# A mixture-of-experts feed-forward by halves of the tokens, with resident weights and shares spread by DMA

## Chip, cores, metric

The kernel runs on one core of a Trainium2 chip. The metric is the device time of one execution in microseconds (us). Before the change it is 1184.66 us, the median of 3 runs (1184.16 to 1185.03).

## What is computed

Four layers act on x of shape 2 x 1024 x 128 (2048 tokens, 128 channels, float32), each added to x and each working on a layer norm of it:

```
x = x + attention(norm(x))      # 16 heads, learned distance bias
x = x + ffn(norm(x))            # F1
x = x + mamba(norm(x))          # x + inner residual
x = x + ffn(norm(x))            # F2, the same weights as F1

ffn(xf):
  scores = sigmoid(xf @ router_w.T)          # 64 experts
  sfc    = scores + correction_bias
  keep the 4 of 8 groups with the best sum of two; the best 8 experts of those
  c      = scores of the chosen / (their sum + 1e-20) * 2.5, zero elsewhere
  routed = sum over e of c[:, e] * (square(relu(xf @ up_w[e])) @ down_w[e])   # hidden 64
  shared = square(relu(xf @ shared_up_w)) @ shared_down_w                     # hidden 256
  return routed + shared
```

Every expert is computed for every token; c is zero for those not chosen.

## The kernel before, in words

Tokens lie in 16 tiles of 128 rows, four quarters of 512. Each layer is a stage (`attention`, `moe_ffn` with the tag f1, `mamba`, `moe_ffn` with f2), with a barrier of all engines between stages. All engines run their own program and wait on semaphores.

**Feed-forward (`moe_ffn`, line 214).** The layer norm (lines 171 to 182) normalizes 16 tiles on VectorE; TensorE transposes them; ACT copies them rounded to fp32r (line 445, the high part) and POOL subtracts to get the low part (line 508). TensorE makes the logits (line 354), ACT the sigmoid (line 451), and VectorE routes all 16 tiles (lines 524 to 567), ending in shares c in two f16 parts, which TensorE transposes to cT (line 388). Meanwhile the two shared pieces run as eight units (lines 457, 461, 365).

The 64 experts are 32 pairs, so that a pair's hidden width is 128. A routed unit is one pair and one quarter, 128 units a stage, in loops of 24 (`each_unit`). In a unit TensorE does three fp32r matmuls up (high x high, low x high, high x low: lines 360 to 362), three down for the unit four back (line 401), and one that spreads the two experts' shares over 64 partitions each, by a one-hot matrix `m.spread` times cT (line 417). ACT does the relu (line 478) and casts the high part of act (line 471); VectorE multiplies relu by the share (line 585) and the product by the hidden value again (line 591), which gives c times the square; POOL subtracts for the low part (line 514). SP loads each pair's weights (lines 320 and 324) into two slots; ACT casts their high parts (lines 484, 492) and VectorE subtracts for the low ones (line 573). So the order in a unit is relu, share product, second product, cast, low part, down.

At the end ACT copies the sums (line 499), TensorE turns them back (line 428), VectorE adds x (line 600) and, in f2, SP stores the output by quarters (line 339).

**Attention (line 752)** goes by steps (ALL_STEPS). SP's queue holds, step by step, the maxima (line 915), tables of the bias and the stacks of q and k; POOL copies v once in a while (line 979). **Mamba**: ACT writes each of 16 units of the projection into a padded buffer (line 1534), VectorE convolves it by three instructions (line 1689); POOL's softplus (lines 1621 to 1627) follows ACT's last copy and VectorE's reciprocal (line 1697).

## Time and profile before

| what | value |
|---|---|
| median of 3 runs | 1184.66 us |
| the profiled execution | 1184.06 us |
| its span | 1182.1 us |
| mean granted TensorE clock | 0.933 |
| busy: TensorE / VectorE / ACT / POOL | 86% / 83% / 61% / 38% |

The span runs from the first instruction to the last; the profiled execution's own time lies 2 us above it. A clock of 1.00 is TensorE's full speed. "Share" of DMA is the mean busy share of the core's 16 DMA engines. All rows are from this one execution. "Idle before" is how long an engine stood still before an instruction, and the name behind the arrow is what ended the wait.

### The profile page before, as it was taken

The page shows a single profiled execution, that of the slowest core. Times are in us where ns is not written, and L with a number is a line of the kernel's source. Part 1 is how long each engine was busy: PE and PEld are TensorE (multiplying, and loading weights), DVE is VectorE, ACT ScalarE, POOL GpSimd, SP SyncE. Part 2 cuts the span into 40 slices and gives each one's busy share as a digit, 9 for nine tenths or more (in the row PEclk, how much of TensorE's full clock was granted, in tenths as well). Part 3 has the DMA queues.
Part 4 walks back from the last instruction along what each step waited for, and adds up shares of the span by engine and source line. Part 5 has one row for each costly group of instructions (what it writes and reads, how often), then busy time and mean ns, then how long its engine had stood idle before and what let it go on. Part 6 is the DMA issues. An engine that isn't in the chain of part 4 may idle for free. (4 is left out here: it accounts for less than half of the span.)

```text
span 1182.1 us, 19693 instructions
## 1 busy us (share of the span) xinstructions
PE 1020.0 (86%) x5756; PEld 540.9 (46%) x5756; DVE 983.5 (83%) x2432; ACT 719.0 (61%) x1175; POOL 447.7 (38%) x404
## 2 busy tenths in 40 slices
PE   3559999999999999785999999782877769999998
PEld 1212222222222222264766676541656537666775
DVE  6589999889999986168999999787876689999997
ACT  5116665666666656564777777586333537777775
POOL 4600000000000000013777778515663127777776
PEclk9659999999999999967999999986889879999999
DMA  3740122032012200000000000000000000000001
GB/s 100 255 95 8 61 76 49 16 106 66 15 55 75 57 1 2 1 21 12 20 21 18 22 18 23 3 19 0 1 0 0 21 9 21 22 18 21 19 23 38
DMA packets 56704, 41.66 MB, mean 35 GB/s; under 512 B 23334, under 2 KB 51004, under 8 KB 56636
## 3 DMA queue, kind: packets, MB, share of 16 engines
q1 hardware_dynamic: 54268, 38.18, 12.0%
q10 hardware_dynamic: 2368, 2.63, 0.8%
q8 instruction: 36, 0.59, 0.2%
q14 instruction: 32, 0.26, 0.1%
HBM read 33.12 MB, written 7.47 MB: 34 GB/s over the span
## 5 line engine op out<-in xcount | busy, mean ns | idle before, releaser
L514 POOL TENSOR_TENSOR f_act_low<-f_act,f_act_high 128x512 fp32r<-128x512 f32 x256 | 331.2, 1294 | 151.3 <-ACT f_act_high L471 146.3
L1203 ACT ACTIVATE at_prob<-at_cols 128x1024 f32<-128x1024 f32 x256 | 248.1, 1021 | 198.4 <-PE at_cols L1092 198.4
L1255 DVE CUSTOM_DVE_ANT_0 at_rows<-at_rows,at_table_max 128x512 f32<-128x512 f32 x512 | 340.3, 719 | 33.5 <-PE at_rows L1057 32.3
L471 ACT CAST f_act_high<-f_act 128x512 fp32r<-128x512 f32 x256 | 159.1, 621 | 68.1 <-DVE f_act L591 65.7
L585 DVE TENSOR_TENSOR f_gated<-f_relu,f_work 128x512 f32<-128x512 f32 x256 | 174.3, 681 | 21.3 <-PE f_work L417 15.1
L591 DVE TENSOR_TENSOR f_act<-f_gated,f_work 128x512 f32<-128x512 f32 x256 | 175.8, 687 | 10.2
L478 ACT ACTIVATE f_relu<-f_work 128x512 f32<-128x512 f32 x256 | 152.9, 597 | 32.1 <-PE f_work L362 30.7
L360 PE MATMUL f_work<-f_x_high,f_wu_high 128*128 128x512 f32 x256 | 148.4, 580 | 2.7 <-DVE f_wu_low L573 2.1
L1057 PE MATMUL at_rows<-at_k_stack,at_q_stack 48*128 48x512 bf16 x512 | 104.7, 405 | 39.9 <-DVE at_maxima L1255 38.4
L1104 PE MATMUL at_pv<-at_prob,at_v_stack 128*32 128x512 f32 x1024 | 136.4, 605 | 0.6 <-ACT at_prob L1203 0.6
L1092 PE MATMUL at_cols<-at_table_cols,flip_sum 128*64 128x512 f16 x1024 | 136.4, 387 | 0.0
L979 POOL COPY at_v_stack<-at_v_nat 128x256 f32<-128x256 f32 x8 | 3.1, 400 | 333.1 <-PE at_pv L1104 333.1
L1057 PEld LDWEIGHTS at_rows<-at_k_stack,at_q_stack 48*128 48x128 bf16 x512 | 24.9, 93 | 189.2 <-DVE at_maxima L1255 150.1
L401 PE MATMUL f_acc<-f_act_high,f_wd_high 128*128 128x512 f32 x256 | 102.2, 399 | 2.4 <-POOL f_act_low L514 2.4
L417 PE MATMUL f_work<-f_cT,spread 128*128 128x512 f16 x256 | 100.9, 394 | 2.5 <-DVE f_gated L585 2.3
L361 PE MATMUL f_work<-f_x_low,f_wu_high 128*128 128x512 f32 x256 | 101.7, 397 | 0.0
L362 PE MATMUL f_work<-f_x_high,f_wu_low 128*128 128x512 f32 x256 | 101.6, 397 | 0.0
L401 PE MATMUL f_acc<-f_act_high,f_wd_low 128*128 128x512 f32 x256 | 101.5, 397 | 0.0
L401 PE MATMUL f_acc<-f_act_low,f_wd_high 128*128 128x512 f32 x256 | 101.5, 396 | 0.0
L1085 PE MATMUL at_cols<-at_q_stack,at_k_stack 51*128 51x512 bf16 x512 | 78.8, 379 | 2.6 <-ACT at_prob L1203 2.6
L1092 PEld LDWEIGHTS at_cols<-at_table_cols,flip_sum 128*64 128x64 f16 x1024 | 49.0, 109 | 63.7 <-issue 38.8
L1255 DVE DVE_READ_ACCUMULATOR2_ANT at_maxima<- 128x1 f32 x512 | 72.8, 142 | 0.0
(274 smaller groups left out, 1393.8 us busy)
## 6 DMA issues: line engine op xcount, KB each, us to landing
at_table_cols<-bias_rows SPq DMA_DIRECT2D x32, 248.0 KB, 5.1
at_table_max<-bias_rows SPq DMA_DIRECT2D x12, 480.0 KB, 4.3
f_wu<-in_L_ffn_up_w_dram SPq DMA_DIRECT2D x64, 64.0 KB, 2.0
f_wd<-in_L_ffn_down_w_dram SPq DMA_DIRECT2D x64, 64.0 KB, 1.8
at_q_stack<-q_parts SPq DMA_DIRECT2D x28, 96.0 KB, 2.4
at_k_stack<-k_parts SPq DMA_DIRECT2D x24, 96.0 KB, 3.9
at_table_max<-bias_rows ACTq DMA_DIRECT2D x4, 480.0 KB, 5.8
k_parts<-at_parts SPq DMA_DIRECT2D x2, 768.0 KB, 5.4
```

Source lines behind the costliest of these rows:

```text
L360: mm(hid[:, n % 3, :], w_hi, xh[:, cols], start=True, stop=False)
L401: last = mm(acc[:, j % 4, :], w[:, slot, :], x[:, j % 4, :], start=False, stop=(k == 2), skip_group_check=True)
L471: nc.scalar.copy(act_h[:, j % 4, :], act[:, j % 4, :]).then_inc(act_high, 1)
L478: nc.scalar.activation(relu[:, j % 2, :], hid[:, j % 3, :], ACT.Relu).then_inc(relu_ready, 1)
L514: nc.gpsimd.tensor_tensor(act_l[:, k, :], act[:, k, :], act_h[:, k, :].bitcast(F32), ALU.subtract).then_inc(act_low, 1)
L585: tt(gated[:, j % 2, :], relu[:, j % 2, :], cw, ALU.mult).then_inc(gate_done, 1)
L591: tt(act[:, j % 4, :], gated[:, j % 2, :], hid[:, j % 3, :], ALU.mult).then_inc(act_ready, 1)
L1057: last = mm(s1[:, (at + j) % SLOTS, :], q_st[r, p.b, p.lh, p.hp, p.lbq * P:(p.lbq + 1) * P], k_st[r, p.b, p.hp, p.mh * BANK:(p.mh + 1) * B ...
L1092: last = mm(s2[u * HALF:(u + 1) * HALF, hp, j, :], m.flip_sum[:], t_col[:, 2 * hp + j, c:c + BANK], start=False, stop=True)
L1104: last = mm(pv[32 * h:32 * h + 32, :], vst[:, it % 2, LT - 1 - s % LT, h, :], prob[:, S % 2, h, :], start=(s % LT == 0), stop=(s % LT == L ...
L1203: act(prob[:, S % 2, 2 * hp:2 * hp + 2, :], s2[:, hp, :, :], ACT.Exp).then_inc(exp_done, 1)
L1255: nc.vector.tensor_tensor_reduce(out=slot, in0=slot, in1=t_max[:, 2 * p.hp + j, c:c + BANK][:, ::-1], scale=1.0, scalar=-3.0e38, op0=ALU.a ...
```

## The change

**Weights.** In attention SP loads all weights of the feed-forward in nine pieces (the shared ones, then eight of four pairs, two DMAs each) into a double buffer, at steps 4, 16, 28 and so on. Two steps later POOL splits each into high and low parts, two copies and two subtractions for a piece. They stay in SBUF for both feed-forward stages. Some of attention's early tensors share their space. The constants `spread` and `ident16` go.

**Halves.** A stage runs two halves of 1024 tokens. Each has a head (norm, logits, routing for 8 tiles), 68 units (34 pairs, the two shared pieces among them, by two quarters) and a tail. The head of half 0 runs alone, on all engines; the head of half 1 is woven into half 0's units at numbered places, the tail of half 0 into half 1's. The programs are written out instead of looped.

**Shares.** c becomes its square root: ACT's Sqrt, then a step of Newton on VectorE. TensorE turns it (four float32 transposes), ACT copies it, SP stores it to DRAM (`c_rows`, one row of 512 tokens for a quarter and an expert). Then each routed unit has one DMA that reads two rows of 2 KB, repeats each over 64 partitions, and writes the 128 x 512 tile `cw` in one of six slots. A slot's load waits for the gate (VectorE's product) six units back; half 1's first six wait for all gates of half 0. VectorE makes max(hidden, 0) times the root of the share in one instruction, ACT squares it and casts the high part, POOL takes the low part. The matmul that spread the shares is gone.

**Mamba.** The padded buffer holds one sequence instead of two, so ACT's copies for the second wait for convolutions of the first; `yg` shares its space with `sz`.

The core of the diff:

```diff
+def allot_weights(m):
+    m.wu_h, m.wu_l = (m.sb(f"wu_{k}", [D, NPAIRS, P], F32R) for k in ("high", "low"))
+    m.wd_h, m.wd_l = (m.sb(f"wd_{k}", [P, NPAIRS, D], F32R) for k in ("high", "low"))
...
+def weave(main, side):
+    side = iter(side)
+    due = next(side, None)
+    for k, _ in enumerate(main):
+        while due is not None and due <= k + 1:
+            due = next(side, None)
+    while due is not None:
+        due = next(side, None)
...
+AT_ROOT, AT_ROWS, AT_TURN, AT_COPY, AT_HIGH, AT_LOW, AT_LOGITS = 2, 3, 5, 6, 7, 8, 8
+AT_SCORE, AT_ROUTE = 12, 13
+AT_C_ROOT, AT_NEWTON, AT_C_TURN, AT_C_COPY = 38, 39, 42, 43
+AT_TAIL = 8
...
+        def sp_shares(sp, b):
+            h = halves[b]
+            sp.wait_ge(h.rcT_ready, 1)
+            sp.dma_start(c_rows[QH * b:QH * (b + 1)].rearrange("q e t -> (q e) t"), rcT[:]).then_inc(h.rc_out, 16)
+            sp.wait_ge(h.rc_out, 16)
+            for n in range(SHARED * QH, FFN_UNITS):
+                k, e = n - SHARED * QH, 2 * (n // QH - SHARED)
+                if k >= C_SLOTS:
+                    sp.wait_ge(h.gate_done, n - C_SLOTS + 1)
+                elif b:
+                    sp.wait_ge(halves[0].gate_done, FFN_UNITS)
+                sp.dma_start(cw[:, k % C_SLOTS, :], c_rows[QH * b + n % QH, e:e + 2, :].unsqueeze(1)
+                             .broadcast_to([2, HID, BANK])).then_inc(h.c_in[k % C_SLOTS], 16)
+                yield
...
+        def pe_units(pe, b):
+            h = halves[b]
+            def up(n):
+                pp, cols = n // QH, slice((QH * b + n % QH) * BANK, (QH * b + n % QH + 1) * BANK)
+                if n == 0:
+                    pe.wait_ge(h.x_low, QH)
+                    if b:
+                        pe.wait_ge(halves[0].gate_done, FFN_UNITS)
+                if n >= 2:
+                    pe.wait_ge(h.gate_done, n - 1)
+                for k, (w, x) in enumerate(((m.wu_h, xh), (m.wu_h, xl), (m.wu_l, xh))):
+                    last = nc.tensor.matmul(hid[:, n % 2, :], w[:, pp, :], x[:, cols], start=(k == 0), stop=(k == 2))
+                last.then_inc(h.up_done, 1)
+            def down(n):
+                pp, s = n // QH, n % PART_SLOTS
+                pe.wait_ge(h.low_done, n + 1)
+                for k, (w, x) in enumerate(((m.wd_h, act_h), (m.wd_h, act_l), (m.wd_l, act_h))):
+                    last = nc.tensor.matmul(acc[:, QH * b + n % QH, :], w[:, pp, :], x[:, s, :],
+                                            start=(pp == 0 and k == 0), stop=(pp == NPAIRS - 1 and k == 2),
+                                            skip_group_check=True)
+                last.then_inc(h.down_done, 1)
+            for n in range(FFN_UNITS + LAG):
+                if n < FFN_UNITS:
+                    up(n)
+                if n >= LAG:
+                    down(n - LAG)
+                yield
...
+        def act_units(a, b):
+            h = halves[b]
+            def high(n):
+                a.wait_ge(h.square_done, n + 1)
+                if n >= PART_SLOTS:
+                    a.wait_ge(h.down_done, n - PART_SLOTS + 1)
+                elif b:
+                    a.wait_ge(halves[0].down_done, FFN_UNITS)
+                nc.scalar.copy(act_h[:, n % PART_SLOTS, :], act[:, n % ACT_SLOTS, :]).then_inc(h.high_done, 1)
+            for n in range(FFN_UNITS):
+                a.wait_ge(h.gate_done, n + 1)
+                if n >= ACT_SLOTS:
+                    a.wait_ge(h.low_done, n - ACT_SLOTS + 1)
+                elif b:
+                    a.wait_ge(halves[0].low_done, FFN_UNITS)
+                nc.scalar.activation(act[:, n % ACT_SLOTS, :], gated[:, n % 3, :], ACT.Square).then_inc(h.square_done, 1)
+                if n:
+                    high(n - 1)
+                yield
+            high(FFN_UNITS - 1)
...
+        def pool_units(pool, b):
+            h = halves[b]
+            for n in range(FFN_UNITS):
+                pool.wait_ge(h.high_done, n + 1)
+                nc.gpsimd.tensor_tensor(act_l[:, n % PART_SLOTS, :], act[:, n % ACT_SLOTS, :],
+                                        act_h[:, n % PART_SLOTS, :].bitcast(F32), ALU.subtract).then_inc(h.low_done, 1)
+                yield
...
+            tt(masked[:], masked[:], wsum[:, 0, :].unsqueeze(2).broadcast_to([P, HT, E_ALL]), ALU.mult).then_inc(h.c_ready, 1)
+            yield AT_NEWTON
+            v.wait_ge(h.root_ready, 1)
+            ch.link(ts(sfc[:], root[:], 1e-18, None, ALU.max))
+            ch.link(nc.vector.reciprocal(sfc[:], sfc[:]))
+            yield AT_NEWTON + 1
+            ch.link(tt(sfc[:], sfc[:], masked[:], ALU.mult))
+            ch.link(tt(sfc[:], sfc[:], root[:], ALU.add))
+            yield AT_NEWTON + 2
+            if b:
+                v.wait_ge(halves[0].rcT_done, 1)
+            ts(rc[:].rearrange("p k a e -> p a k e"), sfc[:].rearrange("p (a k) e -> p a k e", a=QH), 0.5, None,
+               ALU.mult).then_inc(h.rc_ready, 1)
+        def dve_units(v, b):
+            h = halves[b]
+            for n in range(FFN_UNITS):
+                v.wait_ge(h.up_done, n + 1)
+                if n >= 3:
+                    v.wait_ge(h.square_done, n - 2)
+                elif b:
+                    v.wait_ge(halves[0].square_done, FFN_UNITS)
+                if n < SHARED * QH:
+                    ins = nc.vector.tensor_scalar(gated[:, n % 3, :], hid[:, n % 2, :], 0.0, None, ALU.max)
+                else:
+                    k = n - SHARED * QH
+                    v.wait_ge(h.c_in[k % C_SLOTS], 16 * (k // C_SLOTS + 1))
+                    ins = nc.vector.scalar_tensor_tensor(out=gated[:, n % 3, :], in0=hid[:, n % 2, :], scalar=0.0,
+                                                         in1=cw[:, k % C_SLOTS, :], op0=ALU.max, op1=ALU.mult)
+                ins.then_inc(h.gate_done, 1)
...
+        def stage_program(head, units, tail, eng):
+            run(head(eng, 0))
+            weave(units(eng, 0), head(eng, 1))
+            weave(units(eng, 1), tail(eng, 0))
+            run(tail(eng, 1))
...
+                sp.dma_start(rw[:], router_w).then_inc(rw_in, 16)
+                sp.dma_start(cbias[:], correction_bias.rearrange("(a e) -> a e", a=1).broadcast_to([P, E_ALL])).then_inc(cbias_in, 16)
+                run(sp_shares(sp, 0))
+                if out is None:
+                    run(sp_shares(sp, 1))
+                else:
+                    weave(sp_shares(sp, 1), sp_store(sp, 0))
+                    run(sp_store(sp, 1))
+                    for h in halves:
+                        sp.wait_ge(h.stored, 16 * QH)
...
-                def unit(i, j):
-                    slot = j // 4 % 2
-                    if j % 4 == 0:
-                        pe.wait_ge(w_low, 6 * i + (j // 4 + 1))
-                    if past(i, j, 3):
-                        pe.wait_ge(act_ready, BODY * i + (j - 2))
-                    up(wu_h[:, slot, :], wu_l[:, slot, :], j % 4, j)
-                    if past(i, j, LAG):
-                        down_routed(i, j - LAG)
-                    if past(i, j, 1):
-                        pe.wait_ge(gate_done, BODY * i + j)
-                    e = 12 * i + 2 * (j // 4)
-                    mm(cw, m.spread[:, bass.ds(e, 2), :].rearrange("p e j -> p (e j)"),
-                       cT[:, (j % 4) * BANK:(j % 4 + 1) * BANK], start=True, stop=True).then_inc(cw_done, 1)
-                each_unit(pe, unit)
...
-                def unit(i, j):
-                    pair = 6 * i + j // 4
-                    a.wait_ge(up_done, BODY * i + (NS + j + 1))
-                    if past(i, j, 2):
-                        a.wait_ge(gate_done, BODY * i + (j - 1))
-                    nc.scalar.activation(relu[:, j % 2, :], hid[:, j % 3, :], ACT.Relu).then_inc(relu_ready, 1)
...
-                    v.wait_ge(relu_ready, BODY * i + (NS + j + 1))
-                    v.wait_ge(cw_done, BODY * i + (j + 1))
-                    if past(i, j, 2):
-                        v.wait_ge(act_ready, BODY * i + (j - 1))
-                    tt(gated[:, j % 2, :], relu[:, j % 2, :], cw, ALU.mult).then_inc(gate_done, 1)
...
-                    tt(act[:, j % 4, :], gated[:, j % 2, :], hid[:, j % 3, :], ALU.mult).then_inc(act_ready, 1)
-                    if j % 4 == 0 and past(i, j, 4) and not (isinstance(i, int) and pair + 1 == PAIRS):
-                        low_part(wu, wu_h, wu_l, (j // 4 + 1) % 2, w_high, pair + 2, w_low)
-                    if j % 4 == 1:
-                        low_part(wd, wd_h, wd_l, j // 4 % 2, wd_high, pair + 1, wd_low)
...
+WPAIRS = 4
+WCOLS = WPAIRS * P
+WEIGHT_STEPS = tuple(4 + 12 * k for k in range(1 + PAIRS // WPAIRS))
...
+        def load_weights(eng, k):
+            up, down = raw[:, k % 2, 0, :], raw[:, k % 2, 1, :]
+            if k == 0:
+                eng.dma_start(up[:, 0:SHARED * P], shared_up_w).then_inc(raw_in[0], 16)
+                eng.dma_start(down[:, 0:SHARED * P].rearrange("p (s d) -> p s d", s=SHARED),
+                              shared_down_w.rearrange("(s p) d -> p s d", p=P)).then_inc(raw_in[0], 16)
+                return
+            e = 2 * WPAIRS * (k - 1)
+            eng.dma_start(up.rearrange("p (e i) -> p e i", i=HID),
+                          up_w[e:e + 2 * WPAIRS].rearrange("e d i -> d e i")).then_inc(raw_in[k % 2], 16)
+            eng.dma_start(down.rearrange("p (n d) -> p n d", d=D),
+                          down_w[e:e + 2 * WPAIRS].rearrange("(n a) i d -> (a i) n d", a=2)).then_inc(raw_in[k % 2], 16)
...
                         send_maxima(phase_turned_in(S))
+                    if S in WEIGHT_STEPS:
+                        k = WEIGHT_STEPS.index(S)
+                        if k >= 2:
+                            sp.wait_ge(raw_low, 2 * (k - 1))
+                        load_weights(sp, k)
...
+                def split_weights(k):
+                    cut, n = weight_cut(k), P * (SHARED if k == 0 else WPAIRS)
+                    if k == 0:
+                        pool.wait_ge(exp_done, 1)
+                        pool.wait_ge(stored[1], 16 * STORES)
+                        pool.wait_ge(b_lo_out, 64)
+                    pool.wait_ge(raw_in[k % 2], 32 * (k // 2 + 1))
+                    for a, (high, low) in enumerate(((m.wu_h, m.wu_l), (m.wd_h, m.wd_l))):
+                        src = raw[:, k % 2, a, 0:n].rearrange("p (n d) -> p n d", d=P)
+                        nc.gpsimd.tensor_copy(high[:, cut, :], src).then_inc(raw_high, 1)
+                        pool.wait_ge(raw_high, 2 * k + a + 1)
+                        tt(low[:, cut, :], src, high[:, cut, :].bitcast(F32), ALU.subtract).then_inc(raw_low, 1)
+                for S in range(ALL_STEPS):
+                    if S % STEPS == 0 and S >= STEPS and S // STEPS + 1 < ITERS:
+                        pool.wait_ge(pv_done, S)
+                        take_v(S // STEPS + 1)
+                    if S - 2 in WEIGHT_STEPS:
+                        split_weights(WEIGHT_STEPS.index(S - 2))
...
-                    nc.scalar.copy(raw[:, blk, s, CONV - 1 + c0:CONV - 1 + c0 + BANK],
+                    if s:
+                        a.wait_ge(conv_ready, n - 2 * CB + 1 if c0 else CB * (SEQ // BANK - 1) + blk + 1)
+                    nc.scalar.copy(raw[:, blk, CONV - 1 + c0:CONV - 1 + c0 + BANK],
                                    ps[:, 2 + n % 2, :]).then_inc(conv_read, 1)
...
+        yg = sz
```

## Rows read from the trace of the kernel before

**Rows 1.** The page: span, and busy time of each engine.
```profile
span 1182.1 us, 19693 instructions
PE 1020.0 (86%) x5756; PEld 540.9 (46%) x5756; DVE 983.5 (83%) x2432; ACT 719.0 (61%) x1175; POOL 447.7 (38%) x404
```

**Rows 2.** One line of the layer norm: its starts are the starts of three stages.
```profile
L171 DVE TENSOR_TENSOR f_tmp<-x_stats x2: 186/187/188, 502.6 to 920.5; 128x16 f32<-128x16 f32 x2
L171 DVE TENSOR_TENSOR ss_tmp<-x_stats x1: 185/185/185, 767.8 to 767.8; 128x16 f32<-128x16 f32 x1
```

**Rows 3.** Stretches: from:to, length; busy PE, PEld, DVE, ACT, POOL; clock, DMA share, GB/s.
```profile
109.00:499.00 390.00, 374.39 (x2912) 106.85 (x2908) 323.92 (x1026) 240.26 (x256) 2.40 (x6) 1.00 0.17 44
...
919.00:961.00 42.00, 23.98 (x106) 17.02 (x107) 30.24 (x115) 18.45 (x32) 5.62 (x5) 0.76 0.06 15
961.00:1175.00 214.00, 211.58 (x895) 147.58 (x895) 196.32 (x318) 165.08 (x321) 165.64 (x128) 0.99 0.07 19
```

**Rows 4.** Timeline of TensorE, first matmul of one routed unit and of the next.
```profile
1080.67 0.39 PE L417 MATMUL f_work<-f_cT,spread 128*128 128x512 f16 x1
...
1082.30 0.39 PE L417 MATMUL f_work<-f_cT,spread 128*128 128x512 f16 x1
```

**Rows 5.** The chain that ended last, by engine; POOL's and ACT's operations of a unit.
```profile
POOL 11%; issue 9%; PE 1%; POOLq 0%; DVE 0%; ACT 0%; DVEq 0%
...
L514 POOL TENSOR_TENSOR f_act_low<-f_act,f_act_high 128x512 fp32r<-128x512 f32 x256 | 331.2, 1294 | 151.3 <-ACT f_act_high L471 146.3
L471 ACT CAST f_act_high<-f_act 128x512 fp32r<-128x512 f32 x256 | 159.1, 621 | 68.1 <-DVE f_act L591 65.7
...
1080.29 2.69 POOL L514 TENSOR_TENSOR f_act_low<-f_act,f_act_high 128x512 fp32r<-128x512 f32 x2 [0.34 <-ACT f_act_high L471]
```

**Rows 6.** Timeline of the head of F2: start and duration in us.
```profile
932.25 1.02 ACT L451 ACTIVATE f_score<-f_work 128x1024 f32<-128x1024 f32 x1
933.38 1.86 DVE L524 TENSOR_TENSOR f_sfc<-f_score,f_cbias 128x1024 f32<-128x1024 f32 x1 [7.04 <-ACT f_score L451]
...
957.74 1.62 PEld L388 LDWEIGHTS f_work<-ident,f_chl 128*128 128x128 f16 x16 [10.20 <-DVE f_chl L567]
960.67 0.29 PEld L360 LDWEIGHTS f_work<-f_x_high,f_wu_high 128*128 128x128 f32 x1 [1.31 <-DVE f_cT L569]
```

**Rows 7.** The row maxima's DMA: SP's issues (ns), its size, two stretches with it alone.
```profile
L915 SPq DMA_DIRECT2D at_q_stack<-at_negT x32: 698/747/928, 74.6 to 468.1; - x32
...
at_q_stack<-at_negT SPq DMA_DIRECT2D x32, 6.0 KB
...
76.15:76.30 0.15, 0.15 (x2) 0.00 (x0) 0.15 (x1) 0.00 (x0) 0.00 (x0) 0.50 0.19 41
76.98:77.13 0.15, 0.00 (x0) 0.00 (x0) 0.15 (x1) 0.00 (x0) 0.00 (x0) 0.50 0.19 41
```

**Rows 8.** Lines of Mamba and of the shared units: ns, first and last start.
```profile
L1689 DVE SCALAR_TENSOR_TENSOR ss_xc<-ss_raw,ss_cols,ss_xc x48: 655/752/2580, 778.3 to 815.8; 128x512 f32<-128x512 f32 x48
795.00 0.95 ACT L1534 COPY ss_raw<-ss_ps 128x512 f32<-128x512 f32 x1
L1697 DVE RECIPROCAL ss_softplus<-ss_softplus x1: 547/547/547, 807.1 to 807.1; 128x64 f32<-128x64 f32 x1
L180 DVE RECIPROCAL f_tmp<-f_tmp x2: 252/252/252, 504.1 to 921.9; 128x16 f32<-128x16 f32 x2
L461 ACT ACTIVATE f_act<-f_relu x16: 629/632/635, 520.2 to 946.5; 128x512 f32<-128x512 f32 x16
```

**Rows 9.** The stores of the output: their size, and time to landing.
```profile
out_dram<-x_rows SPq DMA_DIRECT2D x4, 256.0 KB, 2.6
```

**Rows 10.** Stretches of attention's start with much DMA; columns as in rows 3.
```profile
25.00:30.00 5.00, 0.00 (x0) 0.00 (x0) 4.93 (x8) 0.00 (x0) 3.92 (x7) 0.94 0.97 349
...
50.00:54.00 4.00, 1.56 (x6) 0.31 (x6) 3.88 (x11) 0.00 (x0) 3.92 (x7) 0.50 1.05 406
65.00:70.00 5.00, 1.92 (x8) 0.41 (x8) 4.82 (x15) 0.00 (x0) 0.00 (x0) 0.50 1.11 235
```

More of the change, by code:

```diff
@@ new lines, in dve_tail @@
+        def dve_tail(v, b):
+            h = halves[b]
+            for j, q in enumerate(quarters(b)):
+                yield AT_TAIL + 2 * j + 1
+                v.wait_ge(h.out_turned, j + 1)
+                rows = m.x[:, QT * q:QT * (q + 1), :].rearrange("p t d -> p (t d)")
+                nc.vector.tensor_tensor(rows, misc[:, j, :], rows, ALU.add).then_inc(h.x_ready, 1)
+                if out is None:
+                    v.wait_ge(h.x_ready, j + 1)
+                    for t in range(QT * q, QT * (q + 1)):
+                        m.row_stats(t).then_inc(h.stats_taken, 1)
+            if out is None:
+                v.wait_ge(h.stats_taken, HT)
@@ L596, in _ @@
-                each_unit(v, unit)
-                for q in range(NQ):
-                    v.wait_ge(out_turned, q + 1)
-                    rows = m.x[:, QT * q:QT * (q + 1), :].rearrange("p t d -> p (t d)")
-                    tt(rows, hid[:, q % 2, :], rows, ALU.add).then_inc(x_ready, 1)
-                    v.wait_ge(x_ready, q + 1)
-                    if out is None:
-                        for t in range(QT * q, QT * (q + 1)):
-                            m.row_stats(t).then_inc(stats_taken, 1)
@@ L605, in _ @@
[L605 to L606 removed]
+                stage_program(dve_head, dve_units, dve_tail, v)
 HEADS = 16
@@ L749, in vector_rows, with attention, pre @@
                                     ALU.subtract, ALU.mult).then_inc(self.norm, 1)
-def attention(m, x, w_in, offsets, amplitudes, sharpness):
+def attention(m, x, w_in, offsets, amplitudes, sharpness, up_w, down_w, shared_up_w, shared_down_w):
     nc = m.nc
     with ExitStack() as stage:
-        m.stage = stage
+        before = ExitStack()
+        m.stage = before
+        def pre(name, shape, dt=F32):
+            return m.sb(f"at_{name}", shape, dt, before)
         def sb(name, shape, dt=F32):
```

574 lines of the change are left out of this document (255 added, 319 removed).

## The prediction

> **What bounds the kernel now.** I read the page's totals first: TensorE is busy 86% of the span, VectorE 83%, an average over four unlike stages [rows 1]. The starts of the layer norms cut the span: attention up to 502.6, the first feed-forward (F1) up to 767.8, Mamba up to 920.5, the second (F2) up to 1182.1; so F1 is 265.2 us, F2 261.6 us, together 526.8 us [rows 2]. The table of stretches then shows two phases in each: a head of some 42 us in which TensorE is busy for 24, and 214 us in which it is busy for 211.6 (rows of F2; F1's are alike) [rows 3]. In the timeline of TensorE one routed unit (512 tokens by one pair of experts) goes from 1080.67 to 1082.30, seven matmuls 0.2325 us apart, with no gap [rows 4]. So TensorE bounds the routed units. The chain of waits names POOL (11%) and "issue" (9%) [rows 5]; that misleads, since POOL, at 1.34 us an operation (two in 2.69 [rows 5]), stands idle in every unit waiting for act_high. The head is bound by the chain norm, logits, sigmoid (ending 933.3), then VectorE's routing, up to the first routed matmul at 960.67 [rows 6]: 24.3 us of routing up to the transposes at 957.74.
>
> **The change, part by part.**
> *Weights.* 18 loads and 36 POOL operations go into attention. POOL is busy for 2.4 of 390 us there [rows 3]; 36 operations at no more than 1.29 us [rows 5] make 46 us. It depends on nothing slower. TensorE, busy 374 of 390 us there, sets the pace, and the DMA engines are at 0.17 [rows 3]. SP has 18 more issues of up to 0.93 us, 17 us among 390 [rows 7]; tables are queued behind them; each waits for a split made 22 steps earlier, which is long done. I take 0; without that cover it could cost 5 us, and a gain has no source.
> *The units.* The seventh matmul goes: 6 x 0.2325 = 1.395 us, 136 units a stage (the shared ones too) instead of 128. VectorE has one instruction in place of two, near 0.75 us by Mamba's of that kind and shape [rows 8]; ACT has the square (0.63) and the cast (0.62), 1.25; POOL 1.34 [rows 5, 8]. If nothing else counted, a unit would take 1.395.
> *The head of half 0* now stands alone ahead of all units. Norm, turn, logits and sigmoid took 12.8 us for 16 tiles (920.5 to 933.3); for eight, 8.8 (the rows of xn, the x parts and the sigmoid halve, the loading of ACT's table stays). Routing 24.3 becomes 15.3: wide operations halve, small ones don't. Added: root 0.7; Newton 6.5, of which the reciprocal of 512 columns is 3.3 (0.547 at 64 against 0.252 at 16 is 6.1 ns a column [rows 8]); turns 0.9 and a copy 0.6. Together 32.8 (8.8 + 15.3 + 0.7 + 6.5 + 0.9 + 0.6); with some waits 33. The store of the shares lands 2.6 us later, as the stores of the output do [rows 9]: 35.6. A load's issue is 0.7, and 1.4 us pass before its engines move: the first share begins to flow at 37.7.
> *The share loads decide.* Each routed unit needs one DMA of 128 rows of 2 KB, 262,144 B, whose source is written as 2 rows x 64 repeats x 512, against 128 partitions. Large transfers here, all with 48 or more as the slowest dimension of both sides, run with all 16 engines busy (share 0.97 to 1.05) at 349 to 406 GB/s [rows 10]. The one kind with a short slowest dimension, 3 on one side and 24 on the other, 6 KB of row maxima (line 915), shows a share of 0.19 and 41 GB/s in both stretches in which it runs: 3 of 16 engines, though it has 24 packets [rows 7]. So engines are dealt out over the slowest dimension, not over packets. The share load's source has 2 there. The trace has no case with the short side on the source alone, so two engines are my reading, not a measurement. Bytes per engine are then 131,072; at 406/16 = 25.4 GB/s this is 5.16 us a unit, at 349/16/0.97 = 22.5 it is 5.83, and were two engines a tenth quicker for having no neighbours, 4.7. I take 5.16, the cleanest row of 2 KB packets.
> The Trainium skill ("DMA: Bandwidth & Descriptors", sections on why a DMA increments its semaphore by 16, and the rules for kernel authors) says that the number of engines is the largest up to 16 that divides the slowest dimension of both patterns, and that a leading short one confines the whole DMA; here that gives 2, and the row with 3 agrees. By its figure of about 27 GiB/s an engine a load would take 4.5 us and the kernel about 1,910 us (an estimate by that page).
> *Sum of one stage.* 37.7 + 64 x 5.16 (330.2) = 367.9. Half 1's first load waits for the last gate of half 0: landing, gate, issue and start, 3 us; another 330.2: 701.1. Behind the last load one unit's chain (gate, square, cast, low part, three matmuls, 4 us) and copy, turns, add and store (6, after [rows 9]): 711. Half 1's head and half 0's tail are hidden in the waits of VectorE; with that cover gone (case B) VectorE's 25 us of a head over 64 units are 0.4 a unit beside 0.75, still under 1.395. The other engines run 1.4 of each 5.2 us; should the clock halve, six matmuls take 2.8, still hidden. The stretch 50 to 54 ran at 0.50 with TensorE a third busy [rows 10].
> *Mamba.* ACT's copy for unit 11 now waits for the eighth convolution. VectorE does 48 instructions from 778.3 on, 0.8 us each, so that is 778.3 + 24 x 0.8 = 797.5, 2.5 us after ACT's copy (795.0) [rows 8]. Behind it on ACT stand four more units and then POOL's softplus; VectorE's convolutions go on to 816 and lose nothing. I take +0.6, between 0 and 2.5.
> *Total.* The profiled execution took 1184.06 us, 0.6 below the median of 1184.66; its span is 1182.1. 1184.1 + 2 x 711 - 526.8 + 0.6 = **2080 us**.
>
> **The rivals.**
> *B, faster:* the loads spread over all 16 engines, since only the packets or the partitions count. A load is then 262,144 B at 349 to 406 GB/s, 0.65 to 0.75 us, hidden below 1.395. A stage is 32.8 + 136 x 1.395 (189.7) + TensorE's woven work 3.6 + 3 at the seam + 2 of stalls + 9 for drain, copies and stores = 240, and the kernel 1184.1 - 526.8 + 480 + 0.6 = 1138. For it: in no row does a short dimension stand on the source alone. Against it: line 915's 24 packets on 3 engines. The point that decides is the pace of loads: a stage bound by them is 50.7 + 128p (37.7, 3 and 10 above), equal to the old 263.4 at p = 1.66 us, or 158 GB/s, 6.2 engines at 25.4. Two are far on the other side.
> *C, the load is slow for another reason:* 16 engines, but 64 reads of one and the same row hold each other up. Nothing in the trace reads a row so. At 130 GB/s, 2.0 us a load, a stage would be 307 and the kernel 1271. Against it: the tables of 65 to 70 us, overlapping short reads of the same rows, still ran at 235 GB/s [rows 10], 1.1 us a load and hidden.
> *D, the loads are quick and yet nothing is gained:* POOL, at 1.34 the nearest below 1.395, is slowed by VectorE's woven head to 1.5 to 1.6 us a unit. A stage would be 254 to 268 (B's sum with 136 units at that pace), the kernel 1166 to 1194. POOL kept 1.29 beside a VectorE that was busy 92% of 214 us [rows 3, 5], so this is unlikely.
>
> **How the numbers follow.** A (two engines) 0.81; B 0.13; C 0.04; D 0.02. Case A's own bounds: pace 4.7 gives 711 - 128 x 0.46 = 652 a stage, 1962 in all, and 5 us less if the head is shorter; pace 5.83 gives 797 a stage, 2252, and 15 more with attention's bound and the head's unknowns. I give 1,950 to 2,270 us. That holds A nearly whole and leaves B, C and D out, 2 in 10. Slower by over 0.2% (which is about what a measurement of this kernel can tell from no change): A, C and a part of D, 0.86; within 0.2%: the middle of D, 0.01; faster: B, 0.13.
>
> **What the profile would show.** Right: during the units a DMA share near 2/16 = 0.125 and about 50 GB/s where 0.07 and 19 stood [rows 3]; one unit each 5.2 us; VectorE's new instruction waiting for the DMA of cw by more than 3 us a unit; TensorE busy 35 to 50% in the stage with a lower clock; F1 and F2 near 711 us; share loads 5 us apart, and landing up to six loads (some 30 us) after issue, since six slots stand in the queue. Attention still ends near 502, with POOL's busy time there some 30 to 45 us up. Head: first gate with a share some 43 us after the stage's start. Wrong: a share of 0.4 or more in the units, or a pace of 1.4 us (B); a share near 1 with a pace of 2 (C). If the pace is 5.2 and the sum still off, the terms at fault are the head and the seam; if the pace lies between, the rate of one engine.

## The result and the profile after

The changed kernel takes 2112.77 us (median of 4 runs, 2111.5 to 2116.83) against 1184.85 in the same series; the ratio is 1.783, with a 95% interval of 1.781 to 1.786. The prediction was 2080 us, within 1,950 to 2,270. The profiled execution took 2116.83 us, with a span of 2115.1.

The page of the changed kernel, lines of totals, the chain that ended last, two groups, and the share load among the DMA issues (these answer to [rows 1, 5, 7]):

```profile
span 2115.1 us, 16927 instructions
PE 1275.4 (60%) x5500; PEld 668.0 (32%) x5500; DVE 814.2 (38%) x2176; ACT 685.8 (32%) x1052; POOL 482.7 (23%) x449
...
DMA 31%; SPq 1%; DVE 1%; PE 1%; ACT 0%; issue 0%; POOL 0%; DVEq 0%; ACTq 0%
...
L588 DVE SCALAR_TENSOR_TENSOR f_gated<-f_hid,f_cw 128x512 f32<-128x512 f32 x256 | 177.0, 692 | 1116.0 <-DMA f_cw<-f_c_rows 1114.0
L473 POOL TENSOR_TENSOR f_act_low<-f_act,f_act_high 128x512 fp32r<-128x512 f32 x272 | 346.2, 1275 | 1078.1 <-ACT f_act_high L437 1078.1
...
f_cw<-f_c_rows SPq DMA_DIRECT2D x256, 256.0 KB
```

No engine is busy for more than 60%, and the reader should look at the last column: VectorE's new instruction (line 588) does 177 us of work and stands idle ahead of it for 1116 us, of which 1114 for the DMA of `cw`. POOL, ACT and TensorE idle behind it in their turn. The chain puts 31% on that DMA and about 1% each on a few engines, and leaves most of the span without a name; as in the kernel before, its shares say less than the wait.

The stretches, with the columns of [rows 3], and the first line of the norm (line 769 now; its first of four starts is F1's):

```profile
109.00:499.00 390.00, 373.14 (x2898) 106.37 (x2890) 329.07 (x1031) 237.58 (x254) 32.09 (x38) 1.00 0.22 55
550.00:880.00 330.00, 171.63 (x405) 108.88 (x405) 61.77 (x132) 77.41 (x134) 82.72 (x65) 0.60 0.13 51
600.00:800.00 200.00, 102.84 (x231) 63.69 (x231) 41.87 (x101) 44.73 (x78) 48.43 (x38) 0.58 0.13 50
...
1237.50:1384.80 147.30, 102.14 (x487) 72.29 (x487) 116.27 (x271) 73.47 (x169) 71.68 (x93) 0.86 0.02 4
...
L769 DVE TENSOR_TENSOR f_tmp<-x_stats x4: 160/166/173, 508.7 to 1418.5; 128x8 f32<-128x8 f32 x4
```

In the units the DMA engines have a share of 0.13 at 50 GB/s: 2 of 16, each at 25 GB/s. The granted clock is 0.60 on average there, between its two levels of 1.2 and 2.4 GHz, and TensorE is busy for 171.6 of 330 us, some 2.8 us a unit: even at the low clock a unit's six matmuls fit in the wait. The stages by their starts: attention 508.7 (502.6 before), F1 from there to 1237.5, 728.8 (265.2), Mamba 147.3 (152.7), F2 from 1384.8 on, 730.3 (261.6). So the two feed-forward stages hold 932 of the 933 us between the spans; attention's 6.1 us more and Mamba's 5.4 less nearly cancel.

The gates of half 0 and the end of F1, from VectorE's and SP's timelines:

```profile
541.29 0.34 SPq L316 DMA_DIRECT2D f_c_rows<-f_rcT  x1
543.34 7.01 SPq L324 DMA_DIRECT2D f_cw<-f_c_rows  x4
550.54 0.69 DVE L588 SCALAR_TENSOR_TENSOR f_gated<-f_hid,f_cw 128x512 f32<-128x512 f32 x1 [0.38 <-DMA f_cw<-f_c_rows]
...
884.10 0.69 DVE L588 SCALAR_TENSOR_TENSOR f_gated<-f_hid,f_cw 128x512 f32<-128x512 f32 x1 [4.57 <-DMA f_cw<-f_c_rows]
...
1225.88 0.69 DVE L588 SCALAR_TENSOR_TENSOR f_gated<-f_hid,f_cw 128x512 f32<-128x512 f32 x1 [4.56 <-DMA f_cw<-f_c_rows]
```

From the first routed gate of half 0 at 550.54 to its last at 884.10 are 63 units: 5.295 us each. This pace makes nearly the whole result.

### The profile page after: what moved, and what is told of

It reads as the page before. It is cut to its first block and busy times, and to the rows that moved or that the text cites. A ratio compares the mean times of both kernels' runs of the same rounds, so it can differ in the third digit from the quotient of the medians.

```text
span 2115.1 us, 16927 instructions
## 1 busy us (share of the span) xinstructions
PE 1275.4 (60%) x5500; PEld 668.0 (32%) x5500; DVE 814.2 (38%) x2176; ACT 685.8 (32%) x1052; POOL 482.7 (23%) x449
## 5 line engine op out<-in xcount | busy, mean ns | idle before, releaser
L588 DVE SCALAR_TENSOR_TENSOR f_gated<-f_hid,f_cw 128x512 f32<-128x512 f32 x256 | 177.0, 692 | 1116.0 <-DMA f_cw<-f_c_rows 1114.0
L377 PE MATMUL f_hid<-f_x_high,wu_high 128*128 128x512 f32 x272 | 190.7, 701 | 620.6 <-DVE f_gated L588 618.3
L444 ACT ACTIVATE f_act<-f_gated 128x512 f32<-128x512 f32 x272 | 171.4, 630 | 1054.2 <-DVE f_gated L588 1029.5
L384 PE MATMUL f_acc<-f_act_high,wd_high 128*128 128x512 f32 x272 | 155.8, 573 | 32.4 <-POOL f_act_low L473 32.4
L384 PE MATMUL f_acc<-f_act_high,wd_low 128*128 128x512 f32 x272 | 159.9, 588 | 0.0
L384 PE MATMUL f_acc<-f_act_low,wd_high 128*128 128x512 f32 x272 | 157.0, 577 | 0.0
L377 PE MATMUL f_hid<-f_x_low,wu_high 128*128 128x512 f32 x272 | 152.5, 561 | 0.0
L377 PE MATMUL f_hid<-f_x_high,wu_low 128*128 128x512 f32 x272 | 152.0, 559 | 0.0
L384 PEld LDWEIGHTS f_acc<-f_act_high,wd_low 128*128 128x128 f32 x272 | 80.7, 297 | 22.4
L384 PEld LDWEIGHTS f_acc<-f_act_low,wd_high 128*128 128x128 f32 x272 | 79.4, 292 | 20.5
```

The lines of the kernel that those rows point to most:

```text
L377: last = nc.tensor.matmul(hid[:, n % 2, :], w[:, pp, :], x[:, cols], start=(k == 0), stop=(k == 2))
L384: last = nc.tensor.matmul(acc[:, QH * b + n % QH, :], w[:, pp, :], x[:, s, :], start=(pp == 0 and k == 0), stop=(pp == NPAIRS - 1 and k == 2),
L444: nc.scalar.activation(act[:, n % ACT_SLOTS, :], gated[:, n % 3, :], ACT.Square).then_inc(h.square_done, 1)
L588: ins = nc.vector.scalar_tensor_tensor(out=gated[:, n % 3, :], in0=hid[:, n % 2, :], scalar=0.0, in1=cw[:, k % C_SLOTS, :], op0=ALU.max, o ...
```

## The experiments

Four theories stood at the start. "Two engines": the load's source has 2 as its slowest dimension, so 2 engines carry it. "Repeated reads": one row read 64 times is slow. "Issue": SP needs that long to issue such a load (its issues show a median of 5.1 us in the trace). And, for what remains once the loads are quick, my own sum of case B, 240 us a stage. The later runs are about that rest.

**The load as two DMAs (e1_two_dmas).**

```diff
-                sp.dma_start(cw[:, k % C_SLOTS, :], c_rows[QH * b + n % QH, e:e + 2, :].unsqueeze(1)
-                             .broadcast_to([2, HID, BANK])).then_inc(h.c_in[k % C_SLOTS], 16)
+                for a in range(2):
+                    sp.dma_start(cw[a * HID:(a + 1) * HID, k % C_SLOTS, :],
+                                 c_rows[QH * b + n % QH, e + a:e + a + 1, :]
+                                 .broadcast_to([HID, BANK])).then_inc(h.c_in[k % C_SLOTS], 16)
...
-                    v.wait_ge(h.c_in[k % C_SLOTS], 16 * (k // C_SLOTS + 1))
+                    v.wait_ge(h.c_in[k % C_SLOTS], 32 * (k // C_SLOTS + 1))
```

> The share load of a unit is written as two DMAs, one for each expert: 64 partitions on the destination, one row repeated 64 times at the source, so that the slowest dimension is 64 on both sides; bytes, packets, rows read and everything else stay. Theory 'two engines': a DMA of this form uses 16 engines, the 256 KB of a unit take about 0.66 us and are hidden, TensorE sets 1.395 us a unit, a stage takes about 240 us, and with attention 508.7 and Mamba 147.3 the kernel ends near 1138 us. Rival 'repeated reads': one row read 64 times is slow whatever the engines; the pace stays at 5.3 us and the time near 2112. Rival 'issue': SP needs 5.1 us to issue a load of 128 packets, since it has so many descriptors to write; two of 64 take the same together, and the time stays near 2112. A weaker form of it: each issue costs 0.7 to 0.9 us, as line 915's do, so two give 1.4 to 1.8 a unit and 1140 to 1220 us.

Measured: 1168.98 us (1166.34 to 1173.65), ratio 0.985 (0.982 to 0.988): 944 us less than the changed kernel, by one edit that leaves the bytes, the packets and the rows read as they were. "Repeated reads" is out. So is the strong form of "issue": the two issues of a unit take 0.6 us each in the median. But 1138 was not reached; a stage takes 258 instead of 240, and the rest of the experiments look for those 18 us.

**More rows at the source (e2_four_rows, e3_eight_rows).** The shares are stored two or four times, and one load reads four or eight rows:

```diff
+COPIES = 2            # 4 in e3_eight_rows
...
-        c_rows = nc.dram_tensor(f"{tag}_c_rows", [NQ, E_ALL, BANK], F32).ap()
+        c_rows = nc.dram_tensor(f"{tag}_c_rows", [NQ, E_ALL, COPIES, BANK], F32).ap()
...
+            for r in range(COPIES):
+                sp.dma_start(c_rows[QH * b:QH * (b + 1), :, r, :].rearrange("q e t -> (q e) t"), rcT[:]).then_inc(h.rc_out, 16)
+            sp.wait_ge(h.rc_out, 16 * COPIES)
...
+                sp.dma_start(cw[:, k % C_SLOTS, :], c_rows[QH * b + n % QH, e:e + 2, :, :]
+                             .rearrange("e r t -> (e r) t").unsqueeze(1)
+                             .broadcast_to([2 * COPIES, HID // COPIES, BANK])).then_inc(h.c_in[k % C_SLOTS], 16)
```

> The shares are stored twice in DRAM, and a unit's single load reads four rows, each repeated over 32 partitions: slowest dimension 4 at the source, 128 packets and 256 KB as before. Theory 'two engines': four engines, so a pace of 5.295 / 2 = 2.65 us; a stage is 51.3 + 128 x 2.65 = 391 us, and one store more for each half, in all near 1441 us; DMA share in the units 0.25. Rivals 'repeated reads' and 'issue': the pace stays near 5.3 and the time near 2112 (repeated reads could gain a little, since each row is read 32 times).

> The same with four copies in DRAM and eight rows, each repeated over 16 partitions. Theory 'two engines': eight engines, 1.32 us a load, just under TensorE's 1.395; a stage near 243 us and the kernel near 1145 us; DMA share about 0.45. Rivals: near 2112.

Measured: 1441.44 us and 1167.07 us. Four rows: 1441 was expected, and the pace is 2.64 us in the trace. Eight rows: 1145 was expected. In the units, with the columns of [rows 3], first four rows, then eight:

```profile
620.00:660.00 40.00, 26.01 (x94) 17.20 (x94) 16.55 (x21) 19.40 (x33) 19.48 (x16) 0.96 0.26 100
```

```profile
690.00:735.00 45.00, 45.00 (x193) 35.82 (x192) 22.26 (x33) 36.55 (x65) 41.51 (x33) 1.00 0.53 194
560.00:600.00 40.00, 36.44 (x140) 24.35 (x139) 34.33 (x85) 27.41 (x49) 30.95 (x24) 1.00 0.44 154
```

Shares of 0.13, 0.26 and 0.53 at 50, 100 and 194 GB/s: two, four and eight engines by the number of rows at the source, with 128 packets each time. At eight TensorE is busy in all of 45 us, at 1.40 us a unit: the new bound of 1.395 is met there. A share at that pace is no count of engines, though, since the loads now wait for TensorE (in e1_two_dmas it is 0.58 in the same 45 us). The packets under 512 B beside the number of loads are a better count. They stand here for the changed kernel (600 to 800), four rows (620 to 660), eight rows and e1_two_dmas (690 to 735):

```profile
DMA packets 4928, 9.99 MB, mean 50 GB/s; under 512 B 76, under 2 KB 76, under 8 KB 4922
f_cw<-f_c_rows SPq DMA_DIRECT2D x38, 256.0 KB
...
DMA packets 2003, 3.99 MB, mean 100 GB/s; under 512 B 60, under 2 KB 60, under 8 KB 2002
f_cw<-f_c_rows SPq DMA_DIRECT2D x16, 256.0 KB
...
DMA packets 4514, 8.74 MB, mean 194 GB/s; under 512 B 269, under 2 KB 269, under 8 KB 4510
f_cw<-f_c_rows SPq DMA_DIRECT2D x32, 256.0 KB
...
DMA packets 5131, 8.46 MB, mean 188 GB/s; under 512 B 1020, under 2 KB 1020, under 8 KB 5127
f_cw<-f_c_rows SPq DMA_DIRECT2D x65, 128.0 KB, 3.0
```

That is 2.0, 3.8, 8.4 and 15.7 small packets (of 4 B) a load, beside packets of 2 KB that carry the shares. I read it as one small packet from each engine that takes part: 2, 4, 8 and 16 engines. In eight rows' stretch 560 to 600 TensorE is not busy all the time: there half 1's head is woven in.

**No loads behind the sixth (e4_no_loads).** `sp_shares` stops after the six slots are filled, and the gate's wait becomes a wait for that one filling.

> Only the first six share loads of each half are made, and the later units use what then stands in the six slots (so most units are weighted by the shares of other experts); all else as changed. It shows what the stage takes without the loads: by my sum of case B about 240 us a stage and 1138 us in all, whatever the theory. If it is near e1_two_dmas, that one's loads are hidden; if it is far above 1138, something else than the loads (POOL at 1.34 us, the woven head on VectorE) binds the units.

Measured: 1238.27 us, a hundred above the expectation, and my fault: the six loads that remain are of the two-engine form. Eight units then take 4.25 us each at the start of half 0 and 3.3 to 3.5 at the seam; a stage is 290 to 295. Everywhere else its units run like those of e3_eight_rows: 1.40 us without the woven head, and 1.6 to 2.1 with it. So it does say that the 18 us are not the loads'.

**Copies in place of POOL's subtractions (e5_pool_copies, e11_attention_copies).** In e5 both edits on e3_eight_rows, in e11 the first alone on the changed kernel. Both leave out the subtraction; the low parts are then copies of the whole values, and only the time counts:

```diff
-                        tt(low[:, cut, :], src, high[:, cut, :].bitcast(F32), ALU.subtract).then_inc(raw_low, 1)
+                        nc.gpsimd.tensor_copy(low[:, cut, :], src).then_inc(raw_low, 1)
...
-                nc.gpsimd.tensor_tensor(act_l[:, n % PART_SLOTS, :], act[:, n % ACT_SLOTS, :],
-                                        act_h[:, n % PART_SLOTS, :].bitcast(F32), ALU.subtract).then_inc(h.low_done, 1)
+                nc.gpsimd.tensor_copy(act_l[:, n % PART_SLOTS, :], act[:, n % ACT_SLOTS, :]).then_inc(h.low_done, 1)
```

> Built on e3_eight_rows. POOL's subtractions of two SBUF tiles become copies of one, for the weights in attention and for act in the units (the low parts are then copies of the whole value, so the matmuls sum other numbers); every wait and every other instruction stays. Theory 'port': VectorE's instructions on SBUF tiles stand still while POOL subtracts, for up to 1.3 us each. Then attention's extra 6 us go (end near 503 instead of 508 to 509), the woven head no longer lengthens the units (1.4 to 1.5 us instead of 1.65 to 2.25), a stage takes 240 to 244 us instead of 257.5, and the kernel ends near 1130 us. Rival 'occupancy': the woven head costs because VectorE has more to do in those units than 1.395 us; then the units stay at 1.65 and more, a stage near 255. Rival 'queue' for attention: the 18 loads delay SP's tables; then attention still ends at 508 to 509.

> The changed kernel itself, with POOL's 18 subtractions in attention replaced by copies (the weights' low parts are then copies of the weights; loads, waits and all else stay, the share loads too). Theory 'port': VectorE's instructions on two SBUF tiles no longer stand still beside them; attention ends at 502 to 503.5 instead of 508.7, Mamba and the feed-forward stages stay at 147, 729 and 730, so the kernel at 2106 to 2111 us against 2112.8. Rival 'queue': the loads in SP's queue are what costs, and attention ends at 508 to 509.

Measured: 1142.46 us for e5, where 1130 was expected; attention 502.1 (505.1 in e3_eight_rows), a stage 246.1 (257). Measured for e11: attention ends at 503.9 instead of 508.7, all else within 0.5 us (2112.18 us). In the changed kernel's timeline VectorE and POOL stand so (start, duration), and over all of attention the two VectorE lines show min, median and max in ns:

```profile
142.58 1.27 POOL L1074 TENSOR_TENSOR wd_low<-at_raw_weights,wd_high 128x512 fp32r<-128x512 f32 x1
142.87 1.13 DVE L1387 TENSOR_TENSOR x_rows<-x_rows,at_onorm 128x128 f32<-128x128 f32 x1
...
L1387 DVE TENSOR_TENSOR x_rows<-x_rows,at_onorm x16: 291/291/1328, 116.9 to 506.1; 128x128 f32<-128x128 f32 x16
L1365 DVE CAST at_negm<-at_mtop x16: 174/174/1126, 71.1 to 471.3; 128x16 bf16<-128x16 f32 x16
```

The same two lines in e11_attention_copies:

```profile
L1387 DVE TENSOR_TENSOR x_rows<-x_rows,at_onorm x16: 291/292/373, 116.5 to 501.2; 128x128 f32<-128x128 f32 x16
...
L1365 DVE CAST at_negm<-at_mtop x16: 174/174/176, 70.8 to 466.5; 128x16 bf16<-128x16 f32 x16
```

An addition of 0.29 us takes 1.13 and ends just behind POOL's subtraction. In the woven head it is the same, here in e3_eight_rows, where POOL subtracts for 1.3 us in every unit:

```profile
L504 DVE TENSOR_TENSOR f_pairA<-f_sfc x4: 424/863/1315, 516.8 to 968.6; 128x256 f32<-128x256 f32 x4
L525 DVE TENSOR_TENSOR f_ahead<-f_gsum x32: 161/188/1306, 519.7 to 980.9; 128x64 f32<-128x64 f32 x4, 128x56 f32<-128x56 f32 x4, 128x48 f32<-128x48 f32 x4, 128x40 f32<-128x40 f32 x4
```

and in e5_pool_copies (its lines are one lower), where POOL's copy takes 0.62 us:

```profile
L503 DVE TENSOR_TENSOR f_pairA<-f_sfc x4: 424/518/614, 513.9 to 953.2; 128x256 f32<-128x256 f32 x4
L524 DVE TENSOR_TENSOR f_ahead<-f_gsum x32: 163/183/362, 516.8 to 961.7; 128x64 f32<-128x64 f32 x4, 128x56 f32<-128x56 f32 x4, 128x48 f32<-128x48 f32 x4, 128x40 f32<-128x40 f32 x4
```

The longest waits shrink with the length of POOL's operation; they don't vanish, which is one reason why "port" expected too much (240 to 244 a stage, 246.1 came). The instructions of VectorE's head add up to 26.6 us where it stands alone; woven in, they are 36.1 us in e3_eight_rows and 27.5 in e5. So VectorE stands still for 8.6 us less, in a stage (F1) that is 10.8 us shorter. Another 1.0 us is gone at the stage's end (10.5 to 9.5), where POOL's shorter operation itself is in the chain. e5 changes both the wait and POOL's own length, and does not divide the gain between them exactly.

Instructions with one input stand still as well. In attention it is the cast of line 1365, in the woven head a TENSOR_SCALAR, here in e3_eight_rows and then, one line lower, in e5_pool_copies:

```profile
L532 DVE TENSOR_SCALAR f_rank<-f_rank x4: 194/717/1239, 522.2 to 982.2; 128x64 f32<-128x64 f32 x4
```

```profile
L531 DVE TENSOR_SCALAR f_rank<-f_rank x4: 194/194/195, 519.2 to 963.5; 128x64 f32<-128x64 f32 x4
```

The Trainium skill ("SBUF — State Buffer", who interferes with whom) states it for two inputs: a VectorE instruction with two SBUF inputs and a GpSimd one that reads SBUF share a port, and the later one stands until the first is through. The two-input rows agree; the cast and the TENSOR_SCALAR are not what this sentence covers.

In attention the direction is clear and the size is not. From the 128th product of probabilities and v to the last, TensorE takes 360.9 to 361.0 us in the four kernels without a subtraction there (the kernel before, e5, e6, e11) and 361.8 to 365.5 in the ten with them; the changed kernel's 365.5 is the longest. The ends of attention spread more: 502.1 and 503.9 with copies, 503.9 to 508.7 with subtractions. e12_no_newton_timed, whose attention is the changed kernel's line for line, ends where e11 does:

```profile
L765 DVE TENSOR_TENSOR f_tmp<-x_stats x4: 161/168/173, 503.9 to 925.2; 128x8 f32<-128x8 f32 x4
```

So the 4.8 us between e11 and the changed kernel can't be taken as the price of 18 subtractions: over the stretch above they cost 1 to 4.5 us, by the execution. "Queue" is out as the main cause: e5 and e11 keep all loads. What e5 leaves of the woven head (by POOL's instructions, units of 1.88 at its start, 2.05 around the reciprocal) I take for occupancy; without the reciprocal (e9, below) the second group falls to 1.52.

**Mamba alone (e6_mamba_only).** The kernel before with the diff's lines for Mamba and no other.

> The kernel before with the change to Mamba alone (one sequence's buffer, the wait for the convolution, the shared tile). My sum: +0.6 us, so 1185. In all kernels with the whole change Mamba took 146 to 150 us instead of 152.7. Theory 'its own': the smaller buffer and the shared tile do that, and Mamba takes 147 here, the kernel 1179. Rival 'placement': the five rounds of the scan's loop cost less because of where the code or the loops of other stages stand; then Mamba takes 153.3 here, the kernel 1185.3, and the convolutions end 1.0 us later than before.

Measured: 1186.67 us, ratio 1.0002 (0.9988 to 1.0016); Mamba takes 153.4 by its starts, 0.7 more than before. In the kernels with the whole change it takes 145.6 to 150.4, so 2 to 7 us less, though its convolutions end 1.0 us later, as in e6; most of that is gained in its loop. The theory of placement is what is left, but nothing tested it.

**Shared units earlier (e7_early_shared).** Six steps of TensorE and four of ACT and VectorE run inside half 0's head:

```diff
+            main = units(eng, 0)
+            for at in head(eng, 0):
+                for _ in range(early.count(at)):
+                    next(main)
+            weave(main, head(eng, 1), len(early))
```

> Built on e3_eight_rows. The four shared units of half 0 run inside the head of half 0, beside the routing, with two routed up-projections behind them, instead of after it. By the steps of my sum for case B the head is a chain on VectorE in which TensorE idles: 4 units of 1.4 us are taken off TensorE's later work, 5.6 us, and up to 2.8 more for the two routed ups; VectorE's chain grows by four gates of 0.45 us, 1.8, and the share store with it. So 4 to 6 us a stage, and 8 to 12 us in all: 1155 to 1159 against 1167. If the first units then wait for the first share load (the store's landing 2 to 3 us, the load's start and flow 2 to 3 us), the gain shrinks to 1 to 2 us a stage.

Measured: 1180.14 us, ratio 0.994 (0.992 to 0.997): 13 us slower than its base (one execution of e3_eight_rows), where 8 to 12 of gain were expected. Two rows of its timeline, then the same two of e3_eight_rows:

```profile
546.66 13.23 SPq L326 DMA_DIRECT2D f_cw<-f_c_rows  x10
551.21 0.69 DVE L591 SCALAR_TENSOR_TENSOR f_gated<-f_hid,f_cw 128x512 f32<-128x512 f32 x1 [10.84 <-DMA f_cw<-f_c_rows]
```

```profile
542.15 17.39 SPq L326 DMA_DIRECT2D f_cw<-f_c_rows  x14
...
546.48 0.67 DVE L591 SCALAR_TENSOR_TENSOR f_gated<-f_hid,f_cw 128x512 f32<-128x512 f32 x1
```

The first routed gate needs the shares back from DRAM, 4.5 us for the four stores and 4.5 for the first load. The four shared units had covered that. Moved forward, they lengthen the chain up to the store (37.8 us from the stage's start instead of 32.6, where 1.8 more was expected), and TensorE waits 10 us behind it. It is the mistake of pricing an idle engine's time without asking what the next wait is.

**The head's long pieces (e8_spread_head, e9_no_newton, e10_both, e12_no_newton_timed).** e8 gives the norm's rows two to a unit and splits the reciprocal in four, with later places for what follows; e9 leaves Newton's step out, so that the share is weighted by ACT's root alone; e10 does both.

```diff
-            ch.link(nc.vector.reciprocal(sfc[:], sfc[:]))
-            yield AT_NEWTON + 1
+            for k in range(HT // 2):
+                yield AT_NEWTON + 1 + k
+                ch.add(nc.vector.reciprocal(sfc[:, 2 * k:2 * k + 2, :], sfc[:, 2 * k:2 * k + 2, :]))
+            ch.sync()
```

> Built on e3_eight_rows. VectorE's two long pieces in the woven head are spread: the eight rows of the norm two to a unit instead of eight at once (2.1 us, 3.8 beside POOL), and the reciprocal of 512 columns (3.35 us) in four pieces, one to a unit; the places of what follows move back by 3 to 10 units. Theory 'long pieces': the groups of eight units at 1.92 us (units 0 to 8) and 2.07 (32 to 40) are long because one piece holds up a gate; they fall to about 1.65, the level of the routing's units, so 5 to 6 us a stage, and 1155 to 1158 in all against 1167. Rival 'each collision': what counts is how many units have some VectorE work on SBUF tiles beside POOL's subtraction; then spreading adds collisions and gives back what it gains, 1163 to 1170.

> Built on e3_eight_rows. The step of Newton is left out (five VectorE instructions, the reciprocal among them; the root is ACT's alone). It prices that term of the head: 0.43 + 3.35 + 0.69 + 0.69, with gaps 5.3 us off the chain of half 0's head, and the same off the woven head of half 1, of which the units at 2.07 us give 3 to 5. So 8 to 10 us a stage, and about 1149 us. If the woven part is bound by the other instructions' collisions with POOL, only 5.3 a stage: 1156.

> The edits of e8_spread_head and e9_no_newton together, on e3_eight_rows: the version that should be quickest. Added up from the two single edits (1167.1 to 1160.2 and to 1145.4): if they are independent, 1138.5; since both shorten the group of units around the reciprocal, which both had as a gain, some 2 to 3 us less gain: 1140 to 1142. Faster than the kernel before by 3.7 to 4%.

> The kernel of e9_no_newton again, timed against the kernel before in five rounds, to tell whether e10_both's spreading adds anything to it. e9 gave 1145.4 in one execution, e10 1148.0 (1144.0 to 1154.9). If spreading gives back by collisions what it gains, this is 1145 to 1149; if it gains on its own, this is 1150 or more.

Measured: e8 1160.22 us, ratio 0.978 (0.975 to 0.981), a stage 253; e9 1145.37, a stage 245.7; e10 1148.04, ratio 0.970 (0.966 to 0.973); e12 1146.63, ratio 0.967 (0.965 to 0.970). e8 lies between its two forecasts: spreading takes the group around the reciprocal from 2.07 to 1.44 us a unit, but the routing's group beside it goes from 1.67 to 1.94. Both theories have a part, and 4 us a stage are gained. Without Newton's step a stage falls by 11.4, more than the 8 to 10 expected: 5.3 off the head that stands alone, 6.1 off the woven one. Spreading adds nothing to that, and the 1140 to 1142 expected of e10 was missed: the two gains don't add up. So e12 is the quickest found that keeps its low parts, 3.3% under the kernel before, with ACT's root unrefined; with Newton's step kept, e8 is, at 2.2% (1.9 to 2.5).

## Why the prediction was right

**The deciding step held.** "I take two engines as my reading, not a measurement" rested on one row of three engines. The DMA share is 0.13 at 50 GB/s, and the count follows the source's rows through 2, 4 and 8. The rule of the Trainium skill ("DMA: Bandwidth & Descriptors", why a DMA increments its semaphore by 16) gives these three counts, and 16 for the 64-row form; the counts of small packets agree, 2.0, 3.8, 8.4 and 15.7 a load. By that page's 27 GiB/s an engine (its specifications) I had estimated a pace of 4.5; it is 5.3, or 24.8 GB/s an engine, and the trace's own row of 2 KB packets was the better price.

**Terms.** The head with the store and the first share: first routed gate predicted some 43 us behind the stage's start, measured 41.8; the store took 2.05 us instead of 2.6, and the first load's packets moved 1.36 us after its issue began, not 2.1. VectorE's chain up to the copy of the shares: 32.8 predicted, 541.3 - 508.7 = 32.6 measured. That this sum met is partly luck: in F1 the part up to the sigmoid took 10.9 (8.8 predicted), the routing 13.4 (15.3), Newton's step 5.7 (6.5). The pace: 5.16 predicted, 5.295 measured, 128 times 0.135 = 17 us a stage; the two stages' 35 us are nearly all of the 37 between 2080 and the profiled execution. I took the rate of a stretch with all 16 engines busy (406 GB/s, share 1.05), 25.4 GB/s an engine; it was 24.8. The share above 1 may have been the hint that a little of that rate was overlap; nothing tested it. The seam: 3 us predicted; loads of half 1 begin at 884.87 and its last gate is at 1225.88, as 64 paces and 2 us give. The end: 10 predicted, 11.6 measured. The sum of a stage, 711 against 729 and 730. One sign was off: TensorE was busy for 52% of the units' time, not 35 to 50.

**Attention: a cost put at nothing.** "It depends on nothing slower" looked at POOL, TensorE, the DMA engines and SP, and not at VectorE, which shares POOL's way to SBUF. Attention ended 6.1 us later, just beyond the bound of 5 that I had given it. The subtractions have a part in it that e5 and e11 show, but not its size: the same attention cost 1.3 to 3.3 us in the nine other kernels that kept it. Mamba: +0.6 predicted, +0.7 measured where it stands alone (e6), but the convolutions did lose 1.0 us where the prediction had them lose nothing; with the whole change Mamba was at -5.4, which no step had. It hid attention's cost in the sum, and that is luck.

**The rivals.** C fell with e1: there a row is still read 64 times, and a unit takes 1.40 us. B's decisive point, 6.2 engines, was right in kind: eight engines end below the kernel before, four far above. Its size was wrong, 1138 against 1167, because of the sentence that VectorE's 25 us of a head over 64 units fit beside 0.75: they are bunched in some 40 units, they stand still beside POOL, and one piece of 3.35 us holds up every gate. D, held unlikely, named this cause (the woven head beside POOL) with the wrong sufferer: POOL kept 1.3 us an operation (1.31 in e3_eight_rows from 547 to 640), VectorE waited.

## What to carry to other kernels

Before a DMA is put in the path of every unit, look at the slowest dimension of both its sides: here a broadcast of two rows was a transfer on two engines, and splitting it in two DMAs, each with 64 outermost, or storing each row four times cured it (twice was not enough, 1441 us). What a tile's spread costs on TensorE (0.23 us here) is to be set against the pace of the transfer that replaces it, not against its bytes over the full bandwidth. And where VectorE's work is woven into a loop in which POOL reads SBUF, an instruction of VectorE on SBUF tiles can take up to POOL's operation more, the two-input ones and here some casts and TENSOR_SCALARs too (0.19 us became 1.24); count that, and look whether pieces longer than a unit's slack can be cut. Cutting gained 4 us a stage here, not the whole.

## What the runs showed that was not expected

SP's issue of a share load takes about as long as a load where the loads set the pace: a median of 5.147 us with two engines and 2.512 with four, but 0.574 with eight. The loads were to stand six deep in the queue and land some 30 us after issue; SP was held at the issue instead, and in the middle of half 0 a load's gate came some 20 us after its issue began. So a slow DMA also holds back whatever is behind it in SP's program.

```profile
L324 SPq DMA_DIRECT2D f_cw<-f_c_rows x256: 501/5147/7977, 543.3 to 2083.6; - x128
```

The output's four stores landed in 6.0 us in the median instead of 2.6 [rows 9]; two of them now stand among the share loads in SP's queue, which is the likely reason and was not tested. And Mamba, whose loop is unchanged, ran 2 to 7 us shorter in all kernels of the changed form; why stays open.
